# Working out a group's row addresses together, ahead of its products, in both layers of a graph network

## The chip, the cores and the metric

The kernel runs on one core of a Trainium2 chip. The metric is the device time of one execution in microseconds. Three runs of the kernel before took 4537.21, 4550.31 and 4554.00 us; the median is 4550.31 us.

## The reference

A graph of 6250 nodes with 128 features and 200,000 edges (`src`, `dst`, sorted by `dst`) goes through two layers. Cut to what matters:

```
# layer 0: mean over a node's edges (self edge with weight 2), then a dense layer
h   = relu(layernorm(x))
msg = concat(h[dst], 2 * h)
red = segment_sum(msg, concat(src, nodes)) / count
x1  = x + relu(concat(red, h) @ kernel + bias)
# layer 1: attention over the edges, 8 heads of 16
h   = relu(layernorm(x1))
q, k, v = h[src] @ Wq.T + bq, h[dst] @ Wk.T + bk, h[dst] @ Wv.T + bv
e   = exp(clip(sum(q * k, per head) / 4, -10, 10))
out = segment_sum(e / (segment_sum(e, src)[src] + 1e-8) * v, src) + h
return x1 + rsqrt(var(out) + 1e-6) * (out - mean(out)) * gamma + beta
```

## The kernel before, in words

Nodes are held as 49 bins of 128, a node's bin being `src // 128` and its lane `src % 128`. Edges are handled 128 at a time (a tile, one edge to a partition). Five engines run in parallel, each through its own written-out list of instructions; semaphores (`wait_ge`, `then_inc`) order them. The order is written by hand, as Python loops.

**Layer 0** (lines 400 to 1170) does two things at once. It sorts the edges by bin, in 13 chunks of up to 122 tiles, and it sums the neighbours of the chunk sorted before. Sorting a chunk takes 21 *place* steps (TensorE L958, 12 products each; DVE prepares each with L643 and L648), *rank* steps (L947, L948, DVE L606), and a few small ones; at its end the table `dst0` of the chunk is known. Then GpSimd (POOL) issues one indirect DMA for each of the 122 tiles (L533), which gathers 128 rows of 386 bf16 numbers from `hk_table` into a ring `got` of 64 tiles. A row holds the value of a node in three bf16 parts, low, middle and high.

The sums go over *cuts*: pairs of tile and bin, 170 to a chunk, 3 to a *group*, 57 groups to a chunk, 729 in all. For a group ScalarE makes one-hot matrices `oh` (L1098, L1104), TensorE multiplies them with the three parts of the gathered rows (`sums`, L1001 to L1003: 9 products) into one of four PSUM banks, and DVE adds each cut into `acc` at its bin (`add`, L765). Which slot of the ring a cut reads is only known at run time: every 8 groups TensorE loads 24 slot numbers into registers (L985), and every product's address is computed from such a register by an instruction of the sequencer that the profile names FUSED_REGOPS. DVE does the same for its bins (`bin0_row`). TensorE waits for the one-hots (`s_oh0`), for the gathered tiles (`s_g`) and for DVE's adds of four groups earlier (`s_a0`).

The gather of a tile waits until the ring's slot is free (`s_m0`, in steps of 4 tiles). A tile can be used by cuts up to 48 further on, so the gather of the 65th tile of a chunk is released by group 17 of the same chunk, and the gathers before it by the last groups of the chunk before. Place steps stand at groups 1 to 31 of a chunk's turn.

Between the layers the nodes are updated and projected (200 us in the profile). **Layer 1** (lines 1450 to 1680) goes over 1611 tiles in 537 groups of 3. POOL gathers keys and values (L1513, into a ring `kv` of 8 groups). TensorE gets the queries of a group with 9 products (`queries`, L1658: a one-hot matrix with the three parts of `q3` at the tile's bin, again with an address from a register, loaded at L1650), DVE multiplies them with the keys (L1533), reduces (L1541), clips (L1547) and weighs the values (L1554), ScalarE takes the exponential (L1626, L1628), TensorE sums over lanes with 3 fp32 products (`sums`, L1669, two passes each), DVE adds into `acc` (L1572). `queries(u + 3)` stands ahead of `sums(u - 2)` in TensorE's list.

Of the kernel before, what the change touches and what calls it, by code (L numbers as in the profile page):

```python
# [18 lines left out]
D = 128  # L19
# [30 lines left out]
G = 3  # L50
# [3 lines left out]
members = lambda k, g: min(G, cuts0(k) - g * G)  # L54
# [25 lines left out]
REGS = 24  # L80
# [18 lines left out]
def build(nc, x, src, dst, k0, b0, wq, bq, wk, bk, wv, bv, gamma, beta, out):  # L99
# [3 lines left out]
    def sbp(phase, name, shape, dt):  # L103
        return phase.enter_context(nc.sbuf_tensor(name, shape, dt))
# [54 lines left out]
    got = sbp(sorting, "got", [P, RING0, ROW], BF16)  # L159
# [12 lines left out]
    with ExitStack() as phase:  # L172
# [8 lines left out]
        with nc.Block() as block:  # L181
            c_pool = Count(sem("s_const"))

            @block.sync
            def _(sp):
                sp.wait_ge(s_pad, 2)
                with nc.allow_non_contiguous_dma("the last edges, one to a partition"):
                    for a, t in ((src, src_i), (dst, dst_e)):
                        sp.dma_start(t[:, 0:FULL], a[0:FULL * P].rearrange("(p c) -> p c", c=FULL))\
                          .then_inc(s_edge, 16)  # L190
                        sp.dma_start(t[0:TAIL, FULL:FULL + 1],
                                     a[FULL * P:N_EDGES].rearrange("(p c) -> p c", c=1)).then_inc(s_edge, 16)
                sp.wait_ge(s_xpad, 1)
                head = (BINS - 1) * P
                sp.dma_start(xs0[:, 0:BINS - 1, :],
                             x[0:head, :].rearrange("(n p) f -> p n f", p=P)).then_inc(s_x, 16)
                sp.dma_start(xs0[0:LAST_NODES, BINS - 1, :], x[head:N_NODES, :]).then_inc(s_x, 16)
# [55 lines left out]
    with ExitStack() as phase:  # L253
# [26 lines left out]
        low = table("low", [P], FP32)  # L280
# [128 lines left out]
        with nc.Block() as block:  # L409
# [492 lines left out]
            def _(t):  # L902
# [74 lines left out]
                regs = {}  # L977

                def sums(k, g):
                    i0 = g * G  # L980
                    u = group0[k] + g
                    if i0 % REGS == 0:
                        t.wait_ge(s_rows, k + 1)
                        n = min(REGS, cuts0(k) - i0)
                        _, regs[0] = nc.values_load_multi_w_load_instructions(  # L985
                            slot_row[0:1, k % 2, i0:i0 + n], engines=[mybir.EngineType.PE], min_val=0,
                            max_val=RING0 - 1, skip_runtime_bounds_check_because="masked to the ring's slots")
                    t.wait_ge(s_oh0, u + 1)

                    m = (g * G + G - 1) // GLOT  # L990
                    if m < len(lots_of(k)):
                        n = lot0[k] + m
                        t.wait_ge(s_g[n % GSEMS], arrived(n))
                    if u >= 4:
                        t.wait_ge(s_a0, added[u - 3])
                    for i in range(members(k, g)):
                        w = oh0[:, u % OHR, i, :]
                        o = total0(u)[:, i * W0:(i + 1) * W0]
                        s = bass.ds(regs[0][(i0 + i) % REGS], 1)
                        row = lambda a, b: got[:, s, a:b].rearrange("p a b -> p (a b)")  # L1000
                        t.matmul(o, w, row(2 * D, 3 * D + 1), start=True, stop=False)  # L1001
                        t.matmul(o[:, 0:D], w, row(D, 2 * D), start=False, stop=False)  # L1002
                        ins = t.matmul(o[:, 0:D], w, row(0, D), start=False, stop=True)  # L1003
                    ins.then_inc(s_m0, 1)

                def pair(u):
# [15 lines left out]
                for i in range(3):  # L1022
                    ins = t.transpose(bank[7][:, i * P:(i + 1) * P], wn[:, i, :], ident[:, :])
# [24 lines left out]
                for k in range(1, CHUNKS + 1):  # L1048
                    n = len(pieces(tiles_of(k), PB)) if k < CHUNKS else 0
                    for g in range(turn_groups(k)):  # L1050
                        if g < groups0(k - 1):
                            sums(k - 1, g)
                        for i in step_at(g, n):
                            place(step0[k] + i)
                            if i == 3 and k + 2 < CHUNKS:
                                counts(k + 2)
                            if i == 4 and k + 2 < CHUNKS:
                                prefix(k + 2)
                            if i == 6 and k + 2 < CHUNKS:
                                block_bounds(k + 2)  # L1060
                            if k + 1 < CHUNKS:
                                rank(k + 1, share(i, n - 1))
                        if n and g == stage_at(n, 0):
                            bins_of_slots(k)
                        if n and g == stage_at(n, 1):
                            turn(k)
                        if n and g == stage_at(n, 2):
                            cut(k)
# [108 lines left out]
    q3 = sbp(layer1, "q3", [P, BINS, 3 * D], BF16)  # L1177
# [290 lines left out]
    with ExitStack() as phase:  # L1468
# [26 lines left out]
        with nc.Block() as block:  # L1495
# [146 lines left out]
            @block.tensor  # L1642
            def _(t):
                regs = {}

                def queries(u):
                    s = u * G
                    if s % REGS == 0:
                        n = min(REGS, GROUPS * G - s)
                        _, regs[0] = nc.values_load_multi_w_load_instructions(  # L1650
                            bin_row[0:1, s:s + n], engines=[mybir.EngineType.PE], min_val=0,
                            max_val=BINS - 1, skip_runtime_bounds_check_because="a count of 48 comparisons")
                    t.wait_ge(s_oT, u + 1)
                    if u >= 3:
                        t.wait_ge(s_prod, u - 2)
                    for i in range(G):
                        for j in range(3):
                            ins = t.matmul(bank[1 + u % 3][:, i * D:(i + 1) * D], ohT[:, u % 4, i * P:(i + 1) * P],  # L1658
                                           q3[:, bass.ds(regs[0][(s + i) % REGS], 1), j * D:(j + 1) * D]
                                           .rearrange("p a b -> p (a b)"), start=(j == 0), stop=(j == 2))  # L1660
                    ins.then_inc(s_q, 1)

                def sums(u):
                    t.wait_ge(s_wgh, u + 1)
                    t.wait_ge(s_of, u + 1)
                    if u >= 3:
                        t.wait_ge(s_a1, (u - 2) * G)
                    for i in range(G):
                        ins = t.matmul(total(u)[:, i * W:(i + 1) * W], oh_f[:, u % 8, i, :],  # L1669
                                       wv_s[:, u % 4, i, :], start=True, stop=True)  # L1670
                    ins.then_inc(s_s, 1)

                for u in range(3):
                    queries(u)
                for u in range(GROUPS + 2):
                    if u + 3 < GROUPS:
                        queries(u + 3)
                    if u >= 2:
                        sums(u - 2)
# [111 lines left out]
```

## Time and profile before

| what | value |
|---|---|
| timed runs, median (lowest, highest) | 4550.31 us (4537.21, 4554.00) |
| profiled execution, span from first to last instruction | 5884.4 us |
| PE busy, with weight loads beside it | 3071.8 us (52%), 2269.0 us (39%) |
| DVE, ACT, POOL busy | 3038.8 (52%), 2089.2 (36%), 3217.7 us (55%) |
| DMA | 490.01 MB, mean 83 GB/s |
| mean granted TensorE clock | 0.616 of full speed |

The profile gives for the profiled execution the span alone, and no time around it. It is 1334 us longer than the median of the timed runs. A group of instructions is shown by its line, engine, operation and tiles; PEld is the weight load of a product, PEldq and DVEq are the sequencers' own instructions, which are not counted as busy. "Idle before" is the engine's idle time ahead of an instruction, with what ended it: another engine's instruction, "issue" (nothing that the profile shows), or "remote" (a semaphore whose setter the profile does not show).

### The profile page before, as it was taken

How to read it: one execution, taken by the hardware profiler on the slowest of the kernel's cores; microseconds unless marked ns; L12 is line 12 of the kernel's file. 1: busy time of each engine (PE TensorE's matmuls, PEld its weight loads, DVE VectorE, ACT ScalarE, POOL GpSimd, SP SyncE). 2: the span in 40 equal slices, each digit the busy share in tenths (PEclk: the TensorE clock that was granted, in tenths of full speed). 3: DMA queues.
4: the chain of work that ended last, by engine and by line, in shares of the span. 5: the costliest groups of instructions: out<-in, count | busy, mean ns of one | idle time of the engine just before them, and what ended most of it. 6: DMA issues, size and time to landing. Idle time of an engine off the chain costs nothing. (4 is left out here: it accounts for less than half of the span.)

```text
span 5884.4 us, 82972 instructions
## 1 busy us (share of the span) xinstructions
PE 3071.8 (52%) x19417; PEld 2269.0 (39%) x19417; DVE 3038.8 (52%) x8517; ACT 2089.2 (36%) x6025; POOL 3217.7 (55%) x3339
## 2 busy tenths in 40 slices
PE   4445445445445455354357555555555555555553
PEld 3324323334334333233234444444444444444442
DVE  7536446445345455354234555555555555555557
ACT  3233333433433333333344333333333333333333
POOL 3464464464564564554634555655555555555564
PEclk9556556556556556566557666666666666666665
DMA  2232232232222322322322333333333333333333
GB/s 80 63 82 53 70 80 55 73 79 55 76 72 56 81 68 57 84 62 61 87 57 68 101 103 100 106 101 102 104 101 105 102 101 105 101 104 103 100 105 63
DMA packets 245464, 490.01 MB, mean 83 GB/s; under 512 B 73156, under 2 KB 155197, under 8 KB 245022
## 3 DMA queue, kind: packets, MB, share of 16 engines
q0 software_dynamic: 153968, 371.50, 24.5%
q1 hardware_dynamic: 90350, 112.89, 6.9%
q8 instruction: 204, 3.34, 0.2%
q14 instruction: 238, 1.95, 0.1%
q10 hardware_dynamic: 704, 0.33, 0.0%
HBM read 468.15 MB, written 56.11 MB: 89 GB/s over the span
## 5 line engine op out<-in xcount | busy, mean ns | idle before, releaser
L533 POOL DMA_INDIRECT got<-hk_table,dst x1563 | 1561.2, 999 | 1325.5 <-PE bank L1003 647.5
L1513 POOL DMA_INDIRECT kv<-kv_table,dst_i x1611 | 1523.0, 945 | 1062.8 <-DVE wv_s L1554 611.4
L765 DVE TENSOR_TENSOR acc<-acc,bank 128x129 f32 x2187 | 634.2, 290 | 1250.2 <-remote 640.9
L1001 PE MATMUL bank<-got,oh 128*128 x2187 | 609.3, 280 | 1170.6 <-DVE acc L765 627.0
L1658 PE MATMUL bank<-q,ohT 128*128 x4833 | 757.8, 263 | 878.4 <-issue 574.6
L1572 DVE TENSOR_TENSOR acc<-acc,bank 128x136 f32 x1611 | 465.4, 289 | 1130.0 <-remote 1070.7
L1669 PE MATMUL bank<-wv_s,oh_f 128*128 128x136 f32 x3222 | 806.6, 401 | 255.5 <-issue 251.1
L1658 PEld LDWEIGHTS bank<-q,ohT 128*128 128x128 bf16 x4833 | 487.9, 101 | 1124.5 <-issue 1018.6
L1104 ACT ACTIVATE oh<-away 128x384 bf16<-128x384 bf16 x733 | 383.1, 523 | 1321.9 <-remote 784.1
L1669 PEld LDWEIGHTS bank<-wv_s,oh_f 128*128 128x128 f32 x3222 | 660.0, 282 | 344.0 <-issue 336.1
L1001 PEld LDWEIGHTS bank<-got,oh 128*128 128x128 bf16 x2187 | 239.9, 110 | 1369.2 <-issue 1317.5
L1098 ACT ACTIVATE away<-iota,negx 128x128 bf16<-128x128 f32 x2187 | 707.2, 386 | 0.0
L1003 PE MATMUL bank<-got,oh 128*128 x2187 | 607.7, 280 | 123.4 <-issue 123.0
L1002 PE MATMUL bank<-got,oh 128*128 x2187 | 607.7, 279 | 117.3 <-issue 114.9
L1605 ACT ACTIVATE oh_f<-oh 128x384 f32<-128x384 bf16 x537 | 274.1, 510 | 1056.5 <-remote 1055.4
L958 PE MATMUL bank<-oh_t,val 128*128 128x128 f16 x3128 | 336.3, 281 | 58.0 <-DVE val L648 32.9
L1626 ACT ACTIVATE wv_s<-att 128x24 f32<-128x24 f32 x537 | 119.6, 223 | 611.5 <-DVE att L1547 345.6
L1611 ACT ACTIVATE off<-lane_r,my_lane 128x384 bf16<-128x384 bf16 x537 | 321.8, 599 | 3.1 <-DMA lane_r<-lane_of_slot 3.1
L958 PEld LDWEIGHTS bank<-oh_t,val 128*128 128x128 f16 x3128 | 286.6, 141 | 75.3 <-DVE val L648 42.0
L1003 PEld LDWEIGHTS bank<-got,oh 128*128 128x128 bf16 x2187 | 242.2, 111 | 181.6 <-issue 148.9
L1002 PEld LDWEIGHTS bank<-got,oh 128*128 128x128 bf16 x2187 | 240.3, 110 | 182.9 <-issue 145.5
L1533 DVE TENSOR_TENSOR prod<-bank,kv 128x384 f32<-128x384 f32 x537 | 292.9, 546 | 29.4 <-remote 28.1
(223 smaller groups left out, 3344.4 us busy)
## 6 DMA issues: line engine op xcount, KB each, us to landing
lane_r<-lane_of_slot SPq DMA_DIRECT2D x269, 192.0 KB
slots_by_bin<-sorted_chunk SPq DMA_DIRECT2D x637, 61.0 KB
kv<-kv_table,dst_i POOLq DMA_INDIRECT x1611
got<-hk_table,dst POOLq DMA_INDIRECT x1563
kv_table<-qkv SPq DMA_DIRECT2D x12, 512.0 KB, 2.9
hk_table<-hk POOLq DMA_DIRECT2D x6, 772.0 KB, 5.3
out<-o SPq DMA_DIRECT2D x12, 256.0 KB
xs<-in_x SPq DMA_DIRECT2D x3, 768.0 KB, 9.7
```

Of the source, the lines that this page charges most:

```text
L533: g.indirect_dma_start(out=got[:, (tile0[k] + t) % RING0, :], out_offset=None, in_=hk_d, in_offset=bass.IndirectOffsetOnAxis(dst0[:, k % 2 ...
L765: v.tensor_tensor(out=o, in0=o, in1=total0(u)[:, i * W0:(i + 1) * W0], op=ALU.add)\
L958: ins = t.matmul(bank[4][:, l * P:(l + 1) * P], val[:, q % 2, l * BLK:(l + 1) * BLK, :, j].rearrange("p w j -> p (w j)"), oh_t[:, q % 2, j ...
L1001: t.matmul(o, w, row(2 * D, 3 * D + 1), start=True, stop=False)
L1002: t.matmul(o[:, 0:D], w, row(D, 2 * D), start=False, stop=False)
L1003: ins = t.matmul(o[:, 0:D], w, row(0, D), start=False, stop=True)
L1098: ins = a.activation(away[:, u % 2, i, :], iota1[:, :], ACT.Abs, scale=1.0, bias=negx[:, k % 2, n:n + 1])
L1104: a.activation(oh0[:, u % OHR, :, :], away[:, u % 2, :, :], ACT.Relu, scale=-1.0, bias=1.0)\
L1513: g.indirect_dma_start(out=kv[:, r, i, :], out_offset=None, in_=kv_d, in_offset=bass.IndirectOffsetOnAxis(dst_i[:, t:t + 1], 0))\
L1572: v.tensor_tensor(out=o, in0=o, in1=total(u)[:, i * W:(i + 1) * W], op=ALU.add)\
L1658: ins = t.matmul(bank[1 + u % 3][:, i * D:(i + 1) * D], ohT[:, u % 4, i * P:(i + 1) * P], q3[:, bass.ds(regs[0][(s + i) % REGS], 1), j * D ...
L1669: ins = t.matmul(total(u)[:, i * W:(i + 1) * W], oh_f[:, u % 8, i, :], wv_s[:, u % 4, i, :], start=True, stop=True)
```

## The change

For a group in layer 0 the nine row addresses of `got` are asked for (`lower_ap`) right after the slot numbers are loaded and ahead of the waits; the products then use them. In layer 1 the same is done for the nine addresses of `q3`. The products, their order, their waits and all other engines' lists stay as they were. The instruction that does register arithmetic takes several operations; before it stood alone ahead of each product, with 2 to 4 operations, and now the 27 operations of a group share five, four with 6 operations and one with 3. TensorE's list has 11394 of them before and 6326 after.

```diff
                             max_val=RING0 - 1, skip_runtime_bounds_check_because="masked to the ring's slots")
+                    row = lambda i, a, b: got[:, bass.ds(regs[0][(i0 + i) % REGS], 1), a:b].rearrange("p a b -> p (a b)")
+                    parts = [(row(i, 2 * D, 3 * D + 1), row(i, D, 2 * D), row(i, 0, D)) for i in range(members(k, g))]
+                    for of_cut in parts:
+                        for part in of_cut:
+                            t.lower_ap(part)
                     t.wait_ge(s_oh0, u + 1)
...
-                        s = bass.ds(regs[0][(i0 + i) % REGS], 1)
-                        row = lambda a, b: got[:, s, a:b].rearrange("p a b -> p (a b)")
-                        t.matmul(o, w, row(2 * D, 3 * D + 1), start=True, stop=False)
-                        t.matmul(o[:, 0:D], w, row(D, 2 * D), start=False, stop=False)
-                        ins = t.matmul(o[:, 0:D], w, row(0, D), start=False, stop=True)
+                        low, mid, high = parts[i]
+                        t.matmul(o, w, low, start=True, stop=False)
+                        t.matmul(o[:, 0:D], w, mid, start=False, stop=False)
+                        ins = t.matmul(o[:, 0:D], w, high, start=False, stop=True)
...
+                    part = lambda i, j: q3[:, bass.ds(regs[0][(s + i) % REGS], 1), j * D:(j + 1) * D]\
+                        .rearrange("p a b -> p (a b)")
+                    parts = [[part(i, j) for j in range(3)] for i in range(G)]
+                    for of_tile in parts:
+                        for p in of_tile:
+                            t.lower_ap(p)
                     t.wait_ge(s_oT, u + 1)
...
-                                           q3[:, bass.ds(regs[0][(s + i) % REGS], 1), j * D:(j + 1) * D]
-                                           .rearrange("p a b -> p (a b)"), start=(j == 0), stop=(j == 2))
+                                           parts[i][j], start=(j == 0), stop=(j == 2))
```

In layer 0, TensorE's list around a group that follows a place and a rank step, before (ISA is the register instruction; lines 1001 to 1003 are the low, middle and high part):

```order
L948 MATMUL bank1<-rows,sel 128x488
L1001 ISA
L1001 MATMUL bank5<-got,oh0 128x129
L1002 ISA
L1002 MATMUL bank5<-got,oh0 128x128
L1003 ISA
L1003 MATMUL bank5<-got,oh0 128x128
...
L1001 ISA
L1001 MATMUL bank6<-got,oh0 128x129
```

The same place of TensorE's list after the change (line 992 asks for the addresses; 1005 to 1007 are the three parts):

```order
L948 MATMUL bank1<-rows,sel 128x488
L992 ISA x5
L1005 MATMUL bank5<-got,oh0 128x129
L1006 MATMUL bank5<-got,oh0 128x128
L1007 MATMUL bank5<-got,oh0 128x128
...
L992 ISA x5
L1005 MATMUL bank6<-got,oh0 128x129
```

The register instructions of a group stand in one block ahead of its first product, and nothing stands between its nine products.

In layer 1, TensorE's list from one group's `sums` to the next, before:

```order
L1669 MATMUL bank4<-wv_s,oh_f 128x136 x3
L1658 ISA
L1658 MATMUL bank2<-q3,ohT 128x128
L1658 ISA
L1658 MATMUL bank2<-q3,ohT 128x128
...
L1669 MATMUL bank5<-wv_s,oh_f 128x136 x3
```

And after:

```order
L1662 ISA x5
L1668 MATMUL bank1<-q3,ohT 128x128 x9
L1678 MATMUL bank4<-wv_s,oh_f 128x136 x3
L1662 ISA x5
L1668 MATMUL bank2<-q3,ohT 128x128 x9
```

The block of five now follows the `sums` products of the group before directly.

## Rows read from the trace of the kernel before

**Rows 1.** The page's head.
```profile
span 5884.4 us, 82972 instructions
```

**Rows 2.** Page, costliest groups: busy us, mean ns, then idle before and its releaser.
```profile
L533 POOL DMA_INDIRECT got<-hk_table,dst x1563 | 1561.2, 999 | 1325.5 <-PE bank L1003 647.5
L1513 POOL DMA_INDIRECT kv<-kv_table,dst_i x1611 | 1523.0, 945 | 1062.8 <-DVE wv_s L1554 611.4
```

**Rows 3.** Timeline, layer 1, flowing: start us, us, engine, line, what, idle before.
```profile
4508.54 0.95 POOL L1513 DMA_INDIRECT kv<-kv_table,dst_i  x1 [0.30 <-issue]
4508.85 0.55 DVE L1533 TENSOR_TENSOR prod<-bank,kv 128x384 f32<-128x384 f32 x1
4509.71 1.26 PE L1658 MATMUL bank<-q,ohT 128*128 x9
4509.80 0.95 POOL L1513 DMA_INDIRECT kv<-kv_table,dst_i  x1 [0.30 <-issue]
4511.56 0.55 DVE L1533 TENSOR_TENSOR prod<-bank,kv 128x384 f32<-128x384 f32 x1
```

**Rows 4.** Timeline, layer 1, in one of the halts.
```profile
4500.92 0.27 PE L1658 MATMUL bank<-q,ohT 128*128 x1 [1.14 <-issue]
4501.63 0.57 PE L1669 MATMUL bank<-wv_s,oh_f 128*128 128x136 f32 x1 [0.45 <-issue]
4503.91 0.30 DVE L1572 TENSOR_TENSOR acc<-acc,bank 128x136 f32 x1 [7.92 <-remote]
```

**Rows 5.** Waits, whole span: who on whom: us in total, times, longest.
```profile
POOL got L533 <- PE bank L1003: 647.5, 51, 68.2
POOL kv L1513 <- DVE wv_s L1554: 611.4, 132, 6.5
```

**Rows 6.** Windows by stage: length, POOL busy (count), PE clock, DMA share, GB/s.
```profile
0.00:126.40 126.40, 39.74 (x61) 0.97 0.27 82
126.40:3010.20 2883.80, 1561.18 (x1563) 0.58 0.27 69
3010.20:3210.60 200.40, 62.72 (x78) 0.68 0.19 57
3210.60:5795.20 2584.60, 1522.96 (x1611) 0.64 0.38 103
5795.20:5884.40 89.20, 31.09 (x26) 0.54 0.20 44
```

**Rows 7.** One line's instructions on TensorE's sequencer: ns lowest/median/highest, first and last start.
```profile
L1001 PEldq FUSED_REGOPS  x2187: 3/60/1394, 220.8 to 3055.7; - x199
L1658 PEldq FUSED_REGOPS  x4833: 3/46/1394, 3214.9 to 5807.1; - x194
```

**Rows 8.** Timeline, layer 0: first and last product of a group that waited for DVE.
```profile
1390.47 0.29 PE L1001 MATMUL bank<-got,oh 128*128 x1 [1.92 <-DVE acc L765]
...
1391.53 0.28 PE L1003 MATMUL bank<-got,oh 128*128 x1
```

**Rows 9.** Timeline, layer 0: first and last product of two groups queued behind place steps.
```profile
1377.66 0.32 PE L1001 MATMUL bank<-got,oh 128*128 x1
...
1378.52 0.31 PE L1003 MATMUL bank<-got,oh 128*128 x1
...
1382.01 0.23 PE L1001 MATMUL bank<-got,oh 128*128 x1
...
1382.47 0.22 PE L1003 MATMUL bank<-got,oh 128*128 x1
```

**Rows 10.** Waits from 1360 to 1408 us, in which POOL waits for group 17.
```profile
ACT oh L1104 <- PE bank L1003: 16.8, 7, 5.7
...
PE bank L1001 <- DVE acc L765: 9.3, 4, 3.5
...
DVE acc L765 <- issue: 5.5, 1, 5.5
...
DVE oh_t L643 <- PE bank L958: 0.5, 1, 0.5
```

**Rows 11.** Timeline, layer 0: DVE's adds of a group.
```profile
1376.29 1.16 DVE L765 TENSOR_TENSOR acc<-acc,bank 128x129 f32 x3 [0.21 <-DVE acc L765]
```

**Rows 12.** All register loads of TensorE in layer 0, as in rows 7.
```profile
L985 PEldq TENSOR_LOAD <-slot_row x103: 17/1621/5689, 218.8 to 3053.9; - x103
```

## The prediction

> **What bounds the kernel now.** I read the page's head and its costliest groups first, then the stretches by stage, then the waits, and last the timeline where the waits are long. The reader should see four things.
>
> First, the profiled execution is no picture of the timed one. Its span is 5884.4 us [rows 1], 1334 us over the timed median of 4550.3. The timeline says where that goes. Every 20 us or so of layer 1 TensorE falls from a product every 0.13 us to one every 0.7 us or slower, waiting for nothing, for some 8 us, while DVE and ScalarE stand still [rows 4]. The gather queue then runs dry behind them, 132 times in layer 1, 611 us in all, 4.6 us each [rows 5]. I counted about 165 recorded TensorE instructions from one halt to the next, whatever they are. I take the halts for a cost of recording, which the timed runs do not have.
>
> Second, between halts layer 1 is set by POOL. A gather takes 0.95 us and the next follows 0.30 us later, three to a group, so 3.75 us a group; the other engines, when they catch up after a halt, do a group in 4511.56 - 4508.85 = 2.71 us, of which the nine products of `queries` are 1.26 us [rows 3]. They have 1.0 us a group to spare.
>
> Third, the same sum explains the timed run. POOL's stage lengths are [rows 6]: 126.4 us ahead of the first gather, 200.4 us from the last gather of layer 0 to the first of layer 1, 89.2 us behind the last. The gathers themselves are 1563 x (0.999 + 0.30) = 2030 us and 1611 x (0.945 + 0.30) = 2006 us [rows 2, 3]. Together 4452 us. The timed median is 98 us more. That is what is left for the waits of the gather queue on other engines, 8 us in each of the 12 or 13 chunks of layer 0.
>
> Fourth, where those 98 us are: in the profile POOL waits for TensorE's L1003 51 times, at most 68.2 us [rows 5]. Most of it is once a chunk, at the 65th tile: it needs group 17 of its own chunk, and the 64 gathers ahead of it (64 x 1.25 = 80 us) are free to run while TensorE does some 34 groups with 11 place steps. Whoever paces these 34 groups is exposed; in the other 23 groups of a chunk the 58 remaining gathers pace everything.
>
> **The change part by part.**
>
> *Register instructions in the group.* Before, each product had one in front, 60 or 46 ns long [rows 7]. A group that has waited runs its nine products over 1391.53 - 1390.47 = 1.06 us, 0.133 us apart [rows 8]. Two groups whose products were already in the queue, so that their register work was done, took 1378.52 - 1377.66 = 0.86 us (0.108 us apart, at the lower clock) and 1382.47 - 1382.01 = 0.46 us (0.058 us, at the higher one) [rows 9]. After the change every group should look like these. So the saving is 0.20 to 0.60 us a group that waited, plus about 0.10 us for the first register instruction, which now comes ahead of the wait; nothing for one that was queued. With a granted clock of 0.58 in layer 0 the lower end is nearer: I take 0.3 us. TensorE then saves 729 x 0.3 = 219 us of layer 0 and at most as much per group in layer 1.
>
> *The block of five.* Five instructions with 27 operations: the row with 4 operations is 60 ns and with 3 is 46, so about 14 ns an operation; four with 6 come to some 88 ns, the last 46, together 0.40 us. Bounds: 0, where TensorE waits anyway or has products queued, and 0.40 us for each group where it does neither. The queue held 12 place products (1.3 us) while a whole group's register work ran, so I take 0. The register loads at L985, up to 5.69 us for 24 numbers [rows 12], stay where they were, and the block follows them as the first register instruction did.
>
> *On the path, layer 1.* Saving 0.3 us of TensorE's group under POOL's 3.75 us: 0. If the cover were gone, 537 x 0.3 = 161 us would be at stake, but the cover is 1.0 us thick. What is late next is POOL again.
>
> *On the path, layer 0.* Of the 729 groups the exposed ones are 34 x 12 = 408, so TensorE saves 408 x 0.3 = 122 us there. How much of it counts depends on who leads. From 1360 to 1408 us, inside one such stretch, TensorE waits for DVE's adds 9.3 us, DVE waits for TensorE 0.5 us and stands 5.5 us in its own register load [rows 10]. DVE's adds alone take 1.16 + 0.21 = 1.37 us a group [rows 11], with the place step's DVE work on top, against TensorE's 1.06 us and its own place work. DVE leads. So most of the 122 us becomes a longer wait of TensorE on DVE. ScalarE does wait for TensorE there (16.8 us), but it works six groups ahead, so a group's wait is no delay of its own. Bounds: 0, and the whole 98 us that the gather queue can win back. I take an eighth of TensorE's saving, 15 us, nearest to the row in which DVE waits 0.5 us in 48, with something for the places where the two alternate around their register loads, and for the last groups, behind the last gather.
>
> *Sum.* 4550 - 15 = 4535 us.
>
> What DVE, ScalarE, POOL and SyncE do is the same as before, so no DMA and no queue is moved.
>
> The row says that products without register work between them run 0.058 us apart. The Trainium skill, "TensorE: Matmul & The Clock Gate", section "Step-by-step: what each phase is for", states that where the sequencer decodes in software it spends about 62 ns on each MATMUL. By that rule a group would cost the sequencer nine times 62 ns plus the block, an estimated 0.96 us, against 1.06 us in the row, and the change would save TensorE a third of what I take; no row here shows the split of decoding from array time.
>
> **The rivals.**
>
> *A. No difference* (forecast above): POOL and DVE set the pace. Own range 4528 to 4565 us.
>
> *B. TensorE leads the exposed stretches.* For it: ScalarE and POOL both wait for L1003 [rows 5, 10], TensorE and DVE are within some tens of per cent of each other, they alternate around loads of up to 5.7 us, and the timed run without halts may have another leader than the profiled one. Against: rows 10. If half of the 122 us count, 4550 - 61 = 4489; the end is 4550 - 98 - 5 (the groups behind the last gather, 17 x 0.3) = 4447 us.
>
> *C. The block is not covered.* Slower: TensorE comes to a group with an empty queue, does 0.40 us of register work that was spread between products before, and the products still run 0.133 us apart, because something else than the register work holds them there. In the 408 exposed groups that is 163 us, of which DVE's lead absorbs about a third and more; 4550 + 50 to 110, so 4600 to 4660 us, I say 4610. It decides if the products stay over 0.12 us apart after a wait. Against: rows 9 show the array taking them faster from the queue.
>
> *D. The change does nothing here*, because most groups in the exposed stretches are queued behind place steps, whose products hide the register work already [rows 9]. That gives 4550 us and falls in the same class as A.
>
> **How the numbers follow.** A measurement of this kernel tells about 0.5% from no change, 23 us: under 4527 is faster, over 4573 slower. A 0.42 and D 0.12 fall within, though A lies only 7 us from the bound and I give a few hundredths of it to either side. B 0.37. C 0.09. Faster 0.38, same 0.53, slower 0.09. The predicted time is A's, 4535 us. For the range: B's lower end is the bound of the unknown, 4447 us, and I leave only a little of it out; above, half of C is left out. 4450 to 4585 us.
>
> **What would show it.** In the changed kernel's profile the nine products of a waited group should take 0.5 to 0.9 us instead of 1.06 us, with none of TensorE's register instructions between them, and 6326 register instructions in all. Gathers in layer 1 should still come 1.25 us apart. TensorE's wait on DVE's adds (L765) should grow by about what its groups shrink; DVE's wait on TensorE should stay small. The profiled span should fall more than the timed runs, for a reason that is no gain: a group of layer 1 has 37 recorded TensorE instructions instead of 41, so 119 halts instead of 132, 13 x 4.6 = 60 us, and something similar in layer 0; I expect 5740 to 5840 us. The prediction is wrong if gathers come closer than 1.25 us, if the waits at the 65th tile shrink by more than the halts explain (B), or if products stay 0.12 us or more apart (C).

## The result, and the profile after

| | median | lowest to highest | runs |
|---|---|---|---|
| kernel before | 4553.46 us | 4537.21 to 4558.64 us | 7 |
| changed kernel | 4533.19 us | 4527.80 to 4534.31 us | 7 |

The changed kernel takes 0.9955 of the time before, 95% interval 0.9945 to 0.9964. That is 20 us less, at the edge of the 0.5% that the prediction called no change, and 2 us from its 4535.

One thing has to be known to read the numbers. The experiments ran on more than one chip, and one of them ran this kernel 29% slower in every run: the kernel before has a median of 5886.78 us there (13 runs, 5871.32 to 5907.25). The profile of before that stands ahead of the prediction [rows 1 to 12] fits that chip, and the times beside it came from a chip like all the others. So for "before" in layer 0 I use below the profile of `l1_only`, a kernel whose layer 0 is that of before, run on an ordinary chip.

The page of the changed kernel, its head and its costliest groups (the columns of [rows 2]; PE is TensorE's products, PEld its weight loads):

```profile
span 4526.1 us, 77904 instructions
PE 2559.3 (57%) x19417; PEld 2157.3 (48%) x19417; DVE 3065.5 (68%) x8517; ACT 2073.7 (46%) x6025; POOL 3290.0 (73%) x3339
L533 POOL DMA_INDIRECT got<-hk_table,dst x1563 | 1629.1, 1042 | 495.5 <-issue 464.0
L1517 POOL DMA_INDIRECT kv<-kv_table,dst_i x1611 | 1523.0, 945 | 491.6 <-issue 488.0
L1005 PE MATMUL bank<-got,oh 128*128 x2187 | 594.0, 281 | 961.3 <-issue 370.5
```

Against [rows 2], nearly all of POOL's idle time ahead of a gather is now "issue", the 0.30 us between two gathers. The profiled execution took 4527.8 us, 1.7 us more than its span: there is no gap between profile and timed runs to explain.

The waits of POOL in the changed kernel, over the whole span:

```profile
POOL got L533 <- PE bank L1007: 28.2, 39, 5.9
POOL kv L1517 <- DVE wv_s L1558: 2.4, 8, 0.3
```

And the stages of the changed kernel, cut as in [rows 6] (length, POOL's busy time and count, clock, DMA share, GB/s), from the first gather on:

```profile
129.40:2249.80 2120.40, 1628.20 (x1563) 0.64 0.37 93
2249.80:2426.90 177.10, 63.64 (x80) 0.73 0.22 65
2426.90:4439.40 2012.50, 1522.06 (x1611) 0.61 0.49 132
4439.40:4526.10 86.70, 32.03 (x27) 0.50 0.27 50
```

Layer 1 is POOL's sum to within 10 us: 1611 x (0.945 + 0.30) = 2006 of 2012.5. In layer 0 the gathers are 1563 x (1.042 + 0.30) = 2098 of 2120.4, and 28.2 us are what is left of POOL's waits for TensorE.

The same from `l1_only`, for before: the group and wait of layer 0's gathers, then the windows of the two layers.

```profile
L533 POOL DMA_INDIRECT got<-hk_table,dst x1563 | 1624.2, 1039 | 526.8 <-issue 458.5
```
```profile
POOL got L533 <- PE bank L1003: 64.4, 57, 9.4
```
```profile
126.10:2272.30 2146.20, 1623.30 (x1563) 0.64 0.37 92
2451.20:4464.00 2012.80, 1522.30 (x1611) 0.59 0.48 132
```

The two spans differ by 24.5 us. Layer 0 is 25.8 us shorter, the rest differs by 3.3 us or less a stage. Within layer 0 POOL's waits for TensorE fell from 64.4 to 28.2 us, the gathers took 4.9 us more and the gaps between them 5.5 us more. A single profile's wait is not that sharp: with the layer 0 of before it is 64.4 and 59.5 us (`l1_only`, `two_before`), with that of the changed kernel 28.2, 42.3 and 39.4 us (the changed kernel, `l0_only`, `two_after`). So it fell by 17 to 36 us.

The products after the change, in the timeline: first, second and last of a group of layer 0 that had waited (start, duration):

```profile
1304.30 0.27 PE L1005 MATMUL bank<-got,oh 128*128 x1 [1.26 <-ACT oh L1108]
1304.36 0.31 PE L1006 MATMUL bank<-got,oh 128*128 x1
...
1305.12 0.31 PE L1007 MATMUL bank<-got,oh 128*128 x1
```

The group's first to last product takes 0.82 us where it took 1.06 [rows 8], and its products stand 0.107 us apart, as the queued ones did [rows 9]. It is a typical one. Over all groups whose first product started more than 0.8 us after the product before it, the median is 1.04 us and the mean 1.06 in `l1_only` (281 groups), and 0.81 and 0.71 us in the changed kernel (346 groups). A quarter of the latter take 0.45 us, at the higher clock, where before 95 in a hundred took 1.02 us or more. The register instructions, as in [rows 7]:

```profile
L992 PEldq FUSED_REGOPS  x3641: 51/74/79, 170.2 to 2273.4; - x192
L1662 PEldq FUSED_REGOPS  x2685: 51/74/74, 2428.0 to 4436.6; - x192
```

An instruction of six operations shows 74 ns, but in the trace those of one block start 0.133 us apart (1331.531, 1331.663, 1331.796, 1331.928, 1332.061 us), the first product 0.2 us behind the last start. A block takes some 0.6 us, not 0.40.

### The profile page after: what moved, and what is told of

Read it like the earlier page. It is cut to its first block and busy times, and to the rows that moved or that the text cites. A ratio compares the mean times of both kernels' runs of the same rounds, so it can differ in the third digit from the quotient of the medians.

```text
span 4526.1 us, 77904 instructions
## 1 busy us (share of the span) xinstructions
PE 2559.3 (57%) x19417; PEld 2157.3 (48%) x19417; DVE 3065.5 (68%) x8517; ACT 2073.7 (46%) x6025; POOL 3290.0 (73%) x3339
## 5 line engine op out<-in xcount | busy, mean ns | idle before, releaser
L533 POOL DMA_INDIRECT got<-hk_table,dst x1563 | 1629.1, 1042 | 495.5 <-issue 464.0
L1005 PE MATMUL bank<-got,oh 128*128 x2187 | 594.0, 281 | 961.3 <-issue 370.5
L1668 PE MATMUL bank<-q,ohT 128*128 x4833 | 552.9, 290 | 778.3 <-DVE prod L1537 735.3
L1668 PEld LDWEIGHTS bank<-q,ohT 128*128 128x128 bf16 x4833 | 435.6, 131 | 918.5 <-issue 541.7
L1005 PEld LDWEIGHTS bank<-got,oh 128*128 128x128 bf16 x2187 | 279.7, 128 | 1079.8 <-issue 887.1
L1678 PEld LDWEIGHTS bank<-wv_s,oh_f 128*128 128x128 f32 x3222 | 699.2, 304 | 9.9 <-DVE wv_s L1558 9.8
L1006 PE MATMUL bank<-got,oh 128*128 x2187 | 605.3, 286 | 0.0
L1007 PE MATMUL bank<-got,oh 128*128 x2187 | 605.1, 287 | 0.0
L958 PE MATMUL bank<-oh_t,val 128*128 128x128 f16 x3128 | 314.5, 272 | 47.1 <-DVE val L648 46.8
L958 PEld LDWEIGHTS bank<-oh_t,val 128*128 128x128 f16 x3128 | 276.5, 140 | 60.4 <-DVE val L648 59.9
L1529 DVE TENSOR_TENSOR oh<-bank,r 128x384 bf16<-128x384 f32 x537 | 295.2, 550 | 8.9 <-ACT bank L1603 6.7
L1007 PEld LDWEIGHTS bank<-got,oh 128*128 128x128 bf16 x2187 | 295.1, 135 | 0.0
L1558 DVE TENSOR_TENSOR wv_s<-kv,bank 128x384 f32<-128x384 f32 x537 | 293.8, 547 | 1.5 <-issue 1.3
```

Of the source, the lines that this page charges most:

```text
L533: g.indirect_dma_start(out=got[:, (tile0[k] + t) % RING0, :], out_offset=None, in_=hk_d, in_offset=bass.IndirectOffsetOnAxis(dst0[:, k % 2 ...
L958: ins = t.matmul(bank[4][:, l * P:(l + 1) * P], val[:, q % 2, l * BLK:(l + 1) * BLK, :, j].rearrange("p w j -> p (w j)"), oh_t[:, q % 2, j ...
L1005: t.matmul(o, w, low, start=True, stop=False)
L1006: t.matmul(o[:, 0:D], w, mid, start=False, stop=False)
L1007: ins = t.matmul(o[:, 0:D], w, high, start=False, stop=True)
```

## Experiments

The theory: the gain is in layer 0 alone, at the few groups for which POOL waits; layer 1 is POOL's, and DVE shares the exposed stretches with TensorE. The main rival: the register work that is saved counts everywhere, or the gain comes from the place of the block rather than its size. Ratios are against the kernel before on the same chip.

### Layer 0 alone (`l0_only`)

The changed kernel with layer 1 as before:

```diff
-                    parts = [[part(i, j) for j in range(3)] for i in range(G)]
-                    for of_tile in parts:
-                        for p in of_tile:
-                            t.lower_ap(p)
```

> The change in layer 0 alone. My theory (the 20 us come from the stretches of layer 0 in which POOL waited for group 17; layer 1 is set by POOL's gathers, 3.75 us a group): 4530 to 4538 us, the whole gain, ratio to before 0.9955. Rival (the gain is in layer 1): no more than 5 us under before. The profile: halts of 8 us in layer 1, as before, since TensorE still records 41 instructions a group there; if the halts come from the number of recorded instructions layer 0 should have about 85 per cent of its halts, if they come from register instructions that stand between products it should have none. Span about 5100 us in the second case.

Measured: 4529.90 us (4517.17 to 4535.36, 5 runs), ratio 0.9949, interval 0.9936 to 0.9963. The whole gain is here, within the noise. What the expectation said of halts could not be seen: this chip has none.

### Layer 1 alone (`l1_only`)

The kernel before with the block in layer 1 and not in layer 0. Against the changed kernel this goes (and the products of layer 0 stay as before):

```diff
-                    for of_cut in parts:
-                        for part in of_cut:
-                            t.lower_ap(part)
```

> The change in layer 1 alone. My theory: no gain, 4550 to 4556 us. Rival: 10 us or more under before. The profile: layer 1 without halts (gathers 1.25 us apart throughout, some 2013 us for its 1611), layer 0 as in the profile before, 2880 us from the first gather to the last.

Measured: 4550.32 us (4547.44 to 4555.86, 11 runs), ratio 1.0001, interval 0.9992 to 1.0011. Layer 1's part gives nothing: 2012.8 us from its first to its last gather, against 2012.5 and 2012.6 in the other two. Again there were no halts. That the profile has none, in a kernel whose layer 0 is untouched, speaks against halts that recording makes on every chip.

### The block behind the waits (`behind_waits`)

```diff
-                    for of_cut in parts:
-                        for part in of_cut:
-                            t.lower_ap(part)
                     t.wait_ge(s_oh0, u + 1)
...
                         t.wait_ge(s_a0, added[u - 3])
+                    for of_cut in parts:
+                        for part in of_cut:
+                            t.lower_ap(part)
```

and likewise in layer 1 behind `s_prod`.

> As the changed kernel, but the block of five register instructions stands behind the group's waits, directly ahead of its first product. If the gain comes from having fewer register instructions and none between the products, the time is the changed kernel's, 4533 us. If it comes from having them ahead of the waits, the group is 5 x 0.13 = 0.66 us later after a wait and its nine products 0.1 to 0.6 us shorter, so nothing is left of the gain or it turns: 4550 to 4565 us. I expect the second in layer 0 and nothing in layer 1: 4550 us.

Measured: 4538.48 us (4531.42 to 4542.40, 6 runs), ratio 0.9974, interval 0.9961 to 0.9988; the changed kernel has 0.9955. POOL's wait on TensorE:

```profile
POOL got L533 <- PE bank L1007: 47.9, 52, 8.7
```

About half of the gain stays when the block is paid behind the wait, more than I expected. The interval lies under 1, so fewer register instructions, with none between the products, are worth something by themselves. That their place ahead of the waits is worth the rest, 9 us, is likely but near the noise: the interval just overlaps those of the changed kernel (0.9945 to 0.9964) and of `l0_only` (0.9936 to 0.9963).

### Addresses cut by cut (`per_cut`)

The three addresses of a cut are asked for ahead of its three products, behind the waits:

```diff
                     for i in range(members(k, g)):
+                        for part in parts[i]:
+                            t.lower_ap(part)
```

> As the changed kernel, but the addresses are worked out cut by cut (in layer 1 tile by tile): two register instructions ahead of each three products, six to a group instead of five ahead of nine products or nine between them. My theory (a waited group's length on TensorE counts a little in layer 0): the group takes about 9 x 0.107 us and twice some 0.1 us for the blocks between, which lie partly under the products of the cut before, so most of the gain stays: 4533 to 4542 us. Rival: what counts is only that the work stands ahead of the waits: 4545 us or more.

Measured: 4535.10 us (4530.39 to 4539.77, 5 runs), ratio 0.9960, interval 0.9947 to 0.9973. Wait and instructions:

```profile
POOL got L533 <- PE bank L1006: 32.0, 37, 8.1
```
```profile
L1002 PEldq FUSED_REGOPS  x4374: 51/62/79, 170.9 to 2279.2; - x199
```

Two instructions a cut (4374 = 2187 x 2), the second and third pair beside the products of the cut ahead, do as well as five ahead of all, as far as the intervals tell. The place alone is not what matters: two instructions behind the wait cost nothing that these runs show.

### DVE's addresses too (`dve_ahead`), and alone (`dve_alone`)

In `add`, DVE's addresses of a group's three adds are worked out together, ahead of its wait; once on the changed kernel, once on the kernel before:

```diff
+                    outs = [acc[:, bass.ds(regs[0][(i0 + i) % REGS], 1), 0:W0].rearrange("p a b -> p (a b)")
+                            for i in range(members(k, g))]
+                    for o in outs:
+                        v.lower_ap(o)
                     v.wait_ge(s_m0, u + 1)
...
-                        o = acc[:, bass.ds(regs[0][(i0 + i) % REGS], 1), 0:W0].rearrange("p a b -> p (a b)")
+                        o = outs[i]
```

> The changed kernel, and in layer 0 DVE's three addresses of a group are worked out together too, ahead of its wait for the products: two register instructions for six operations or more instead of three between the adds. My theory that DVE leads the exposed stretches: POOL still waits 28 us for TensorE in the changed kernel, so up to that much is to be had: 4510 to 4530 us. Rival (TensorE led and is now out of the way, POOL sets everything): 4531 to 4535 us, no difference.

> The kernel before, with nothing changed on TensorE, and DVE's addresses of a group in layer 0 worked out ahead of its wait. In the run that had both, they gave 60 us, and TensorE's part alone gave 20. If DVE leads the exposed stretches and TensorE follows, DVE's part alone gives about 40 us or more: 4505 to 4515 us. Rival (the two alternate, so that each is worth something only once the other is out of the way): under 20 us, 4530 us or more.

Measured: both together 4490.87 us (4489.34 to 4492.45, 4 runs), ratio 0.9869, interval 0.9854 to 0.9884; DVE's part alone 4522.00 us (4514.76 to 4535.44, 6 runs), ratio 0.9938, interval 0.9922 to 0.9954. So TensorE's part is worth 20 us, DVE's 29, and both together 60. That is 11 us more than the sum of 49, and the three intervals (4 us either way on the 20, 7 on each of the others) leave as much open, so it is not shown that the two edits help each other. The small edit on DVE gives as much as the large one on TensorE or more (the intervals overlap), and the kernel with both is the fastest here that leaves nothing out.

None of the forecasts came. With both edits the time lies under 4510 to 4530 us, and the rival's "no difference" is further off. DVE's part alone lies between "40 us or more" and "under 20 us".

In the timeline of the version with both, DVE's three adds of a group, beside 1.16 us before [rows 11]:

```profile
1404.23 0.93 DVE L769 TENSOR_TENSOR acc<-acc,bank 128x129 f32 x3
```

Its gathers and POOL's wait, over the whole span:

```profile
L533 POOL DMA_INDIRECT got<-hk_table,dst x1563 | 1609.7, 1030 | 482.9 <-issue 463.4
```
```profile
POOL got L533 <- PE bank L1011: 15.6, 41, 1.8
...
PE bank L1009 <- DVE acc L769: 263.8, 153, 6.2
```

And the same two of DVE's part alone:

```profile
L533 POOL DMA_INDIRECT got<-hk_table,dst x1563 | 1607.1, 1028 | 514.6 <-issue 460.0
```
```profile
POOL got L533 <- PE bank L1007: 51.1, 52, 8.0
```

With DVE's part POOL's wait falls (64.4 to 51.1, and 28.2 to 15.6 us), and the gathers get shorter as well (1624.2 to 1607.1, and 1629.1 to 1609.7 us). All profiles with DVE's list as before have 1620.0 to 1629.1 us of gathers on the ordinary chips, the three with DVE's part 1607.1 to 1613.2. So about half of what DVE's part gives comes from shorter gathers, and this is what the forecast from 28 us of waits left out. TensorE's part shortens POOL's waits alone.

The kept traces show which gathers these are. In the changed kernel 476 of the 1563 gathers of layer 0 overlap one of DVE's instructions L643, L648 and L554, which work for the sorting. They take 1.262 us on average. The other 1087 take 0.946 us, as in layer 1, also where they overlap DVE's adds. So all of the 150 us by which layer 0's gathers exceed 0.946 us each lie in the 476. With both edits it is 488 gathers of 1.215 us, 131 us in all, and again 0.946 us for the others. The sorting instructions are the same in both kernels, so with DVE's part they lengthen the gathers less. Why they lengthen them at all, and why less then, no run shows.

### Layer 1 with less work for POOL (`two_after`, `two_before`)

From the ninth group of layer 1 on the gather of a group's third tile is left out (the old contents of its place are used), on the changed kernel and on the kernel before:

```diff
-                    for i in range(G):
+                    for i in range(G if u < RING1 else G - 1):
...
-                    v.wait_ge(s_gk[u % RING1], 16 * G * (u // RING1 + 1))
+                    v.wait_ge(s_gk[u % RING1], 16 * (G + (G - 1) * (u // RING1)))
```

> The changed kernel, with the third of the three gathers of each group of layer 1 left out from the ninth group on (its products go on with old rows), so POOL needs 2.5 us a group instead of 3.75. My theory: POOL sets layer 1, so it gets shorter until the next engine sets it: DVE's group of 2.7 us, 537 x (3.75 - 2.7) = 560 us less, about 3970 us. Rival (layer 1 is set by DVE, TensorE or the landing of gathers): less than 300 us.

> The kernel before, with the same gathers of layer 1 left out. It tells what the change would be worth in layer 1 without POOL's cover. If DVE sets the group there too: the difference to the changed kernel with the same gathers left out stays the 20 us of layer 0, about 3990 us. Rival (TensorE's 1.24 us for nine products and 1.4 us for the other three come to DVE's 2.7 us, so the change frees it): 50 to 160 us slower than the changed kernel's. Its profile should show the halts of 8 us in layer 1 if they come from how dense TensorE's recorded instructions are.

Measured: 3996.74 us (3989.95 to 3998.27, 4 runs), ratio 0.8776, interval 0.8762 to 0.8790, and 4021.90 us (4018.86 to 4030.20, 4 runs), ratio 0.8840, interval 0.8825 to 0.8855. The windows of layer 1, changed and before (length, then busy time and count of PE, PEld, DVE, ACT and POOL, clock, DMA share, GB/s):

```profile
2425.80:3909.60 1483.80, 1009.90 (x7970) 894.21 (x7971) 1414.88 (x4236) 890.31 (x2664) 1021.30 (x1082) 0.77 0.52 132
```
```profile
2449.00:3933.70 1484.70, 1196.92 (x7968) 956.54 (x7968) 1415.09 (x4235) 889.71 (x2663) 1021.35 (x1081) 0.85 0.52 132
```

Two things are shown. With a third of its gathers gone, layer 1 is 529 us shorter: POOL set it, and the cover over the others is 3.75 - 2.76 = 1.0 us a group, as the prediction had it (2.71 us, so 560 us and 3970 us, were forecast for this run). And without that cover the change is worth 0.9 us in all of layer 1: DVE is busy 1415 of 1484 us. TensorE's products take 187 us less, and at a lower clock (0.77 against 0.85), and the stage is no shorter for it. So layer 1's edit is hidden twice. The profiles of the two kernels differ by 24.1 us: 19.4 lie between the first and the last gather of layer 0, and 3.5 between the layers.

### The halts (`again`)

The kernel before, unchanged, profiled once more.

> The kernel before once more, unchanged, for its profile. All six profiles since then are free of halts, also of kernels that record 41 TensorE instructions a group in one layer or the other. If the halts belong to the kernel before (all its register instructions between products, in both layers), this profile has them again and a span near 5880 us. If they were an accident of that one profile, its span is near its own timed time, 4550 us. I expect the second.

Measured: 5889.17 us, with a span of 5887.4. The recorded time is the time that it took, and 13 timed runs on the same chip have a median of 5886.78 us. My expectation, an accident of that profile, was wrong, and so was the prediction's first step. By then nine profiles, and not six, were free of halts, and all nine were of other chips. Each timed run has a span recorded with it too, so how long the kernel takes on this chip when nothing at all is recorded no run shows. Gathers and waits of this run, beside [rows 2, 5]:

```profile
L533 POOL DMA_INDIRECT got<-hk_table,dst x1563 | 1567.0, 1003 | 1324.2 <-PE bank L1003 666.4
```
```profile
POOL got L533 <- PE bank L1003: 666.4, 56, 68.0
POOL kv L1513 <- DVE wv_s L1554: 606.3, 132, 5.7
```

A halt in its timeline, TensorE alone:

```profile
4501.18 0.22 PE L1658 MATMUL bank<-q,ohT 128*128 x1 [1.04 <-issue]
4502.58 0.27 PE L1658 MATMUL bank<-q,ohT 128*128 x1 [1.18 <-issue]
4503.28 0.27 PE L1658 MATMUL bank<-q,ohT 128*128 x1 [0.44 <-issue]
```

One instruction every 0.7 us, a register instruction and a product together 1.4, as in [rows 4]. Register instructions of SyncE take 0.7 us there too (145 of 637, median of all 37 ns); DVE's stay at 57 ns.

### Register loads from an aligned row (`even_rows`, `best`, `rows_of_176`)

The loads at L985 take 1.62 us or up to 5.69 us for 24 numbers [rows 12]. The rows are 173 numbers of 4 bytes, so each second row begins 692 bytes in. `even_rows` is the changed kernel with rows of 174, `best` adds DVE's part to it, `rows_of_176` is changed kernel, DVE's part and rows of 176:

```diff
-        slot_row = sbp(phase, "slot_row", [1, 2, INC], I32)
-        bin0_row = sbp(phase, "bin0_row", [1, 2, INC], I32)
+        slot_row = sbp(phase, "slot_row", [1, 2, INC + 1], I32)
+        bin0_row = sbp(phase, "bin0_row", [1, 2, INC + 1], I32)
```

> The changed kernel, with the rows of slot and bin numbers from which TensorE and DVE load their registers in layer 0 made one number longer (174 instead of 173), so that the second of the two rows begins at a multiple of 8 bytes. In every second chunk a load of 24 numbers takes 5.68 us, in the others 1.62 us. If the row's place in memory is what makes the difference, all full loads should take 1.62 us, and 42 loads on each of the two engines get 4.06 us shorter, 170 us an engine; where POOL has the cover it is worth nothing, in the exposed stretches up to the 28 us that POOL still waits: 4505 to 4530 us. Rival: the difference is something else (what DVE or the DMAs do in odd chunks), and the loads stay at 5.68 us.

> The changed kernel, with DVE's addresses of a group in layer 0 worked out ahead too, and with the longer rows. DVE's part gave 40 us; the rows add what is left of POOL's waits in layer 0, 16 us and a little for gathers that DVE's work no longer stretches: 4465 to 4485 us. If POOL alone sets layer 0 by now: 4488 us.

Both ran on the slow chip, against 5886.78 us for before: 5864.69 us (5853.91 to 5880.43, 8 runs), ratio 0.9955, interval 0.9938 to 0.9973, and 5832.44 us (5822.91 to 5843.01, 6 runs), ratio 0.9902, interval 0.9882 to 0.9923. Rows that begin 696 bytes in do not help: in `even_rows` the longest load is what it was, and one of layer 1's waits tells of the halts:

```profile
L985 PEldq TENSOR_LOAD <-slot_row x103: 533/1622/5699, 221.2 to 3046.7; - x103
```
```profile
POOL kv L1517 <- DVE wv_s L1558: 600.2, 132, 4.9
```

So `even_rows` is in effect the changed kernel on the slow chip, and its ratio there is the same 0.9955, 22 us. In `best` the longest load is 5.70 us as well, so it is in effect `dve_ahead` on that chip: 54 us less than before, where `dve_ahead` had 60, and a ratio of 0.9902 against 0.9869. Both forecasts of faster loads missed. Layer 1 of `even_rows` has 37 recorded TensorE instructions a group instead of 41, but the 132 waits are still 132, one for four groups. The prediction's count of instructions between halts does not hold.

> The changed kernel, with DVE's addresses worked out ahead in layer 0 as well, and the rows from which both engines load their registers 176 numbers long, so that the second row begins at a multiple of 64 bytes (704) from the first; with 174 numbers (696 bytes) its loads still took 5.68 us. All loads of layer 1 begin at multiples of 32 bytes and take 1.62 us. If it is a matter of 16 bytes or more, every full load takes 1.62 us now and the time is 5 to 30 us under that of DVE's part without it (4491 us where the kernel before takes 4551): 4465 to 4486 us, ratio to before 0.981 to 0.9856. If the odd chunks' loads are slow for another reason, they stay at 5.68 us, and the ratio is 0.987. On a chip on which the kernel before takes 5887 us, the ratios are smaller than that: 0.985 to 0.990.

Measured on an ordinary chip: 4500.88 us (4494.37 to 4502.58, 4 runs), ratio 0.9877, interval 0.9860 to 0.9895. Loads, gathers and waits of this kernel:

```profile
L989 PEldq TENSOR_LOAD <-slot_row x103: 545/1617/1824, 166.5 to 2236.7; - x103
```
```profile
L533 POOL DMA_INDIRECT got<-hk_table,dst x1563 | 1613.2, 1032 | 481.8 <-issue 463.4
```
```profile
POOL got L533 <- PE bank L1011: 14.7, 41, 2.5
PE bank L1009 <- DVE acc L769: 122.1, 106, 5.7
```

With rows 704 bytes apart no load takes longer than 1.82 us, and all of TensorE's loads together fall from 323.6 to 153.4 us. TensorE's wait on DVE falls from 263.8 us (`dve_ahead`) to 122.1. The time is no better, 0.9877 against 0.9869 with overlapping intervals, and not in the forecast 0.981 to 0.9856, because POOL's gathers are nearly the whole of the stage: 1563 x (1.032 + 0.30) = 2082 of 2090 us. POOL's wait had only 15.6 us left to give, and kept 14.7.

## Why the prediction came out, step by step

**The time was right, 4535 against 4533.19 us, and so was the class of no difference, at its edge.** Several of the steps behind it were not, and that the time came within 2 us is in part luck: the 15 us were chosen between 0 and 98, and the median of before moved by 3 us.

**The halts are a cost of recording: wrong.** This was the first step, and `again` refutes it: the timed runs on that chip are as long as the profiled one. The profile of before was of a chip that runs the kernel 29% slower; its timed runs were of another. The inference from a gap between profile and timed runs to a cost of recording had a second reading, another chip, which I did not weigh. I escaped most of its consequences since I took the gathers' own durations and left the halts out, but not the one on who leads (below). The profiled span forecast from it, 5740 to 5840 us, was 4526.1.

**POOL sets layer 1, with 1.0 us of cover: right.** 2012.5 us measured and 2006 worked out; `l1_only` 1.0001; two gathers a group bring it to 2.76 us a group, where [rows 3] gave 2.71.

**98 us of waits in layer 0: mis-sized.** An ordinary chip shows 64.4 us. The gathers there are longer, 1.039 us, so they take 1563 x 1.339 = 2093 us and not 2030; the stretch between the layers is shorter, 178.9 us and not 200.4 [rows 6]. The sum hid both behind one remainder. The waits were also spread, 57 of at most 9.4 us, and not one long one a chunk.

**Saving per waited group 0.20 to 0.60 us, 0.3 taken: right.** The means of the waited groups are 1.06 and 0.71 us, 0.35 less; the medians 1.04 and 0.81. Over layer 0 TensorE's products are busy 180 us less (1286.1 to 1105.9), where 219 were forecast. The Trainium skill, "TensorE: Matmul & The Clock Gate", section "Step-by-step: what each phase is for", gives about 62 ns of sequencer time for a MATMUL where it is decoded in software, and I worked out an estimate of 0.96 us from it, block included. The trace does not bear it out: the quickest waited groups of the changed kernel run their nine products in 0.45 us, 0.056 us apart. Whether this chip decodes in software no run shows. Nothing else here depends on it.

**The block at 0.40 us: mis-sized, about 0.6 us.** The durations of the register instructions were near the mark (74 ns for the estimated 88), but they do not follow one another at once. Behind the waits, where nothing hides it, it cost some 9 us (`behind_waits`). How much of it is hidden ahead of the waits no run separates. Rival C, in which products stay over 0.12 us apart, did not happen.

**DVE leads, an eighth of TensorE's 122 us counts: the size near, by luck; the reason only in part right.** 20 us came where 15 were forecast, but the eighth was picked and not worked out. "DVE leads" was read from 48 us of the slow chip's profile [rows 10]. In all of that profile TensorE waits 627.0 us for DVE and DVE 116.5 us for TensorE; on an ordinary chip it is 347.0 and 217.9 us (`l1_only`). In layer 0 (130 to 2270 us) there, before (`l1_only`):

```profile
PE bank L1001 <- DVE acc L765: 344.5, 147, 5.4
PE bank L1001 <- issue: 236.7, 66, 5.8
DVE acc L765 <- PE bank L1003: 210.0, 89, 10.5
```

After:

```profile
PE bank L1005 <- issue: 370.5, 103, 10.1
PE bank L1005 <- DVE acc L765: 368.9, 206, 5.8
DVE acc L765 <- PE bank L1007: 201.2, 86, 10.1
```

Over the 2140 us each waits for the other in turn, and DVE's wait on TensorE is not small, though it was forecast to stay so. TensorE's wait on DVE should have grown by about what its groups shrink. It grew by 24 us, and the products shrank by 180. Most of the rest stands as idle time "issue" before a group's first product, 236.7 to 370.5 us. It is not the register loads: ahead of the 103 groups that load registers TensorE idles 299 us in both kernels, ahead of the other groups 528 us before and 663 after. Part of it may be the block, which the page does not count as busy; what the rest waits for the profile does not show.

## What to carry to other kernels

Whether a saving counts is read from the engine that sets the stage, here POOL, and its time has two parts: what it waits and what its own instructions take. Its wait on TensorE, 64 us of 4550, was what TensorE's edit could win, and it won 20. It was no bound on DVE's edit, which gave some 40 us on top of a kernel with 28 us of such waits left, in part since the gathers themselves got shorter. Where two engines hand banks to and fro, try the cheap edit on each: the one on the engine that the first change left alone brought at least as much. When a profile's span and the timed median differ by a third, compare profiled and timed runs of one chip before explaining the difference.

## What the runs showed of the hardware

- One chip ran this kernel at 5887 us where others took 4551 to 4557, in each of 13 timed runs. In it TensorE slows to an instruction every 0.7 us for some 8 us, once for four groups of layer 1. What the edits save is much the same there: 22 and 54 us, against 20 and 60. The cause is open.
- A register instruction with six operations shows 74 ns but takes 0.133 us from start to start. With one register instruction ahead of each product a waited group of nine took 1.02 us or more; without them 0.81 us at the lower clock and 0.45 us at the higher.
- A load of 24 numbers into TensorE's registers takes 1.62 us from the first row and from a second row that begins 704 bytes in, and 5.7 us from a second row at 692 or 696 bytes. No other distance was run.
- The same kind of indirect gather holds POOL 1.028 to 1.042 us on average in layer 0 and 0.945 in layer 1. The whole excess lies in gathers that overlap DVE's f16 instructions L643, L648 and L554 (476 of 1563 in the changed kernel, 1.262 us on average, against 0.946 for the others). One of them:

```profile
1385.99 0.95 DVE L648 TENSOR_TENSOR val<-pw,oh_j 128x1536 f16<-128x1536 f16 x1
1386.20 1.56 POOL L533 DMA_INDIRECT got<-hk_table,dst  x1 [0.30 <-issue]
```
